# Window attention on one core: row sums and reciprocals behind the value products, row groups innermost

## The reference, cut to what matters

```
x   = x + depthwise3x3(x) + pos_b                      # B, 16, 512, 512
y   = affine1(x) in windows of 8 x 8 pixels            # 16384 windows of 64 tokens, 16 channels
qkv = y @ qkv_w.T + qkv_b ; 2 heads of 8 channels ; q *= 8 ** -0.5
attn = softmax(q @ k.T, axis=-1)                       # 64 x 64 for each window and head
out  = (attn @ v) @ proj_w.T + proj_b
x    = x + out
x    = x + gelu(affine2(x) @ fc1_w.T + fc1_b) @ fc2_w.T + fc2_b    # 64 hidden channels
```

## Time and profile before

| | us |
|---|---|
| median of 3 runs | 33319.02 (33314.83 to 33333.28) |
| the profiled execution's own time | 33304.16 |
| its span, first to last instruction | 33302.7 |
| attention stage, up to its last table load | about 7773 of the span |
| PE, DVE, ACT, POOL busy in the whole span | 30263.7, 27134.7, 24424.2, 11786.8 |

### The profile page before, as it was taken

How to read it: one execution, slowest core, us unless ns; L and a number is a source line. 1 busy time by engine, 2 the same in 40 slices (tenths; PEclk the granted TensorE clock), 3 DMA queues, 4 the chain that set the end, 5 groups by cost and what they waited for, 6 DMA issues and landing times. The chain is left out here.

```text
span 33302.7 us, 708247 instructions
## 1 busy us (share of the span) xinstructions
PE 30263.7 (91%) x264406; PEld 14087.6 (42%) x264406; DVE 27134.7 (81%) x28269; ACT 24424.2 (73%) x25873; POOL 11786.8 (35%) x10892
## 2 busy tenths in 40 slices
PE   7888888889998998999899899899989989989999
PEld 5555555554443343343343333343333434433333
DVE  8888888888997998899799799799889979963102
ACT  5666666667997998899799799799889979951010
POOL 2222222223443443444344344344434434431000
PEclk7777777779999999999999999999999999999999
DMA  1111111116998999999899899899999989999757
GB/s 23 20 20 20 19 20 20 20 20 123 175 175 165 175 175 170 169 175 175 165 175 176 165 175 176 165 175 175 174 166 175 175 165 175 175 241 342 234 183 246
DMA packets 2325306, 4877.21 MB, mean 146 GB/s; under 512 B 632480, under 2 KB 764576, under 8 KB 2322464
## 3 DMA queue, kind: packets, MB, share of 16 engines
q0 software_dynamic: 1224320, 3655.97, 61.4%
q1 hardware_dynamic: 945184, 923.44, 10.2%
q10 hardware_dynamic: 154112, 270.62, 2.2%
HBM read 745.98 MB, written 497.03 MB: 37 GB/s over the span
## 5 line engine op out<-in xcount | busy, mean ns | idle before, releaser
L871 PE MATMUL surf_ps<-surf_u,surf_matf 64*64 64x512 f32 x184960 | 20187.8, 594 | 1619.2 <-ACT surf_Cc L918 555.0
L871 PEld LDWEIGHTS surf_ps<-surf_u,surf_matf 64*64 64x64 f32 x184960 | 8267.0, 134 | 13540.9 <-issue 13534.6
L975 POOL DMA_DIRECT2D surf_u<-surf_ds x4080 | 3452.9, 1154 | 3677.5 <-DVE surf_ds L1038 3295.5
L429 POOL TENSOR_TENSOR att_pr<-att_pr,att_rs 128x1024 f32<-128x1024 f32 x1024 | 2083.9, 2055 | 5660.5 <-DVE att_rs L500 5660.5
L1179 PE MATMUL conv_ps<-conv_rows,conv_w 128*96 128x512 f32 x8256 | 3555.1, 593 | 162.9 <-DVE conv_rows L1200 110.9
L1045 DVE SCALAR_TENSOR_TENSOR surf_rH<-surf_Hc,surf_dt_ab,surf_rH 128x1024 f32<-128x1024 f32 x1360 | 1747.1, 1285 | 1955.8 <-ACT surf_rH L901 1556.5
L953 POOL DMA_DIRECT2D surf_Hc<-surf_m x1360 | 1739.2, 1279 | 3668.8 <-DMA surf_Hc<-surf_Ha 3159.3
L968 POOL DMA_DIRECT2D surf_nK<-surf_B x1360 | 1327.5, 976 | 4088.6 <-ACT surf_B L930 3886.9
L926 ACT ACTIVATE surf_p2q<-surf_pq 128x2048 f32<-128x2048 f32 x1360 | 2591.8, 1906 | 133.0 <-DVE surf_pq L1010 126.8
L471 DVE SCALAR_TENSOR_TENSOR att_acc<-att_xin,att_vec,att_acc 128x512 f32<-128x512 f32 x2048 | 2464.2, 1203 | 45.4
L206 PE MATMUL att_t<-att_ident,att_pr 128*128 128x128 f32 x8192 | 1621.7, 331 | 888.7 <-ACT att_pt L329 886.2
(11 more groups left out here) (88 smaller groups left out, 47547.7 us busy)
## 6 DMA issues: line engine op xcount, KB each, us to landing
surf_p2q<-surf_p2q POOLq DMA_DIRECT2D x1360, 512.0 KB, 10.7
surf_Hc<-surf_Ha POOLq DMA_DIRECT2D x1360, 512.0 KB, 12.3
surf_nK<-surf_B POOLq DMA_DIRECT2D x1360, 512.0 KB, 11.7
surf_Hc<-surf_m POOLq DMA_DIRECT2D x1360, 512.0 KB, 9.0
surf_u<-surf_ds POOLq DMA_DIRECT2D x1360, 256.0 KB, 5.4
surf_u<-surf_ds POOLq DMA_DIRECT2D x2720, 128.0 KB, 7.8
conv_rows<-hidden SPq DMA_DIRECT2D x688, 256.0 KB, 4.0
hidden<-conv_outs ACTq DMA_DIRECT2D x688, 192.0 KB, 4.7
```

Source lines behind the costliest of these rows:

```text
L429: pool.tensor_tensor(pr[:, rg], pr[:, rg], rs[:, rg, :].unsqueeze(2).to_broadcast([P, WC * HEADS, N]), ALU.mult).then_inc(norm_done[rg], 1)
L871: mm = pe.matmul(ps[out, t, :], matf[rows, mat, :], u[rows, k, t, off + 2:off + 2 + W], start=(i == 0), stop=(i == len(taps) - 1))
L975: pool.dma_start(u[rows, k, t, 2:W + 2].rearrange("p a w -> p (a w)"), ds[found, t, :], accum_op=ALU.add).then_inc(u_added, 16)
```

## The change

It takes the normalisation of the attention out of the way of the transposes. The transposed `pt` now holds exp without the division; PE forms the row sums from `pt` by products with a constant 0/1 matrix `pick`, ACT forms 1/sum as exp(-ln(sum)), and DVE multiplies the value products by it. DVE's `total` and all of GpSimd's work are gone, the value products stand in one run with the row group innermost, `pt` has room for two whole chunks, `out_rows` for two stores, the loop body holds four slots, and the order of the steps on PE, ACT and DVE is a new one. The bias of the values goes through the projection once, ahead of the loop (`b_out`).

```diff
-        mx, sm, rs = sb("mx", [P, RG, WC * HEADS]), sb("sm", ...), sb("rs", ...)
-        pt = sb("pt", [P, 2, WC, P])
+        mx = sb("mx", [P, RG, WC * HEADS])
+        pt = sb("pt", [P, 2, RG, WC, P])
+        pick = sb("pick", [P, 2, P // RG])
+        rec = sb("rec", [P, T])
-        out_rows = sb("out_rows", [P, WS, 2 * CW])
+        out_rows = sb("out_rows", [P, 2, WS, 2 * CW])
-        TURNS = [(1, 0), (0, 0), (0, 1), (1, 1), (3, 0), (2, 1), (2, 0), (3, 1)]
+        TURNS = [(1, 0), (0, 0), (0, 1), (1, 1), (3, 1), (2, 1), (3, 0), (2, 0)]
# every_slot
-            for i in range(-2, 5):
-            with eng.Fori(5, CHUNKS - 3, 2) as i:
+            for i in range(-2, 9):
+            with eng.Fori(9, CHUNKS - 3, 4) as i:
+                for k in range(4):
+                    slot(i + k, (1 + k) % 4)
# PE
             def turn(i, rg, half):
-                pe.wait_ge(norm_done[rg], i + 1)
+                pe.wait_ge(exp_done[rg], i + 1)
-            def values(i, par, p):
-                pe.wait_ge(t_copied, i * 8 + (p * 4 + 4))
+            def values(i, par):
+                pe.wait_ge(t_copied, i * 8 + 8)
+                pe.wait_ge(v_split, i + 1)
+                wait(pe, o_done, i)
                 for w in range(WC):
                     for r in range(2):
-                        for rg in (2 * p, 2 * p + 1):
+                        for rg in range(RG):
                             mm = pe.matmul(ps_o[32 * rg:32 * rg + 32, w * N:(w + 1) * N],
                                            vx[:, par, r, w, rg].rearrange("p a h d -> p (a h d)"),
-                                           pt[:, rg % 2, w, r * N:(r + 1) * N], start=(r == 0), stop=(r == 1))
+                                           pt[:, par, rg, w, r * N:(r + 1) * N], start=(r == 0), stop=(r == 1))
+            def sums(i, par):
+                pe.wait_ge(t_copied, i * 8 + 8)
+                after(pe, (gelu_done[1], i - 1), (k_split, i + 1))
+                for r in range(2):
+                    for rg in range(RG):
+                        mm = pe.matmul(ps_mm[32 * rg:32 * rg + 32, 0, :], pick[:, r, :],
+                                       pt[:, par, rg, :, r * N:(r + 1) * N], start=(r == 0), stop=(r == 1))
+                mm.then_inc(den_made, 1)
+            def slot(i, turn4):          # PE, the new order
+                value(i - 1, o); turn(i - 1, 2, 1); scores(i, par, 0); fc1(i - 2, par, 0)
+                turn(i - 1, 3, 0); fc1(i - 2, par, 1); turn(i - 1, 2, 0); scores(i, par, 1)
+                sums(i - 1, o); turn(i, 1, 0); values(i - 1, o); turn(i, 0, 0)
+                project(i - 1); turn(i, 0, 1); fc2(i - 2, par); turn(i, 1, 1)
+                query(i + 1, o); turn(i, 3, 1); key(i + 1, o)
# ACT
-            def move_o(i):               # o_sb = ps_o + bias
+            def reciprocals(i):
+                act.wait_ge(den_made, i + 1)
+                wait(act, o_done, i)
+                act.activation(rec[:, :], ps_m[0], ACT.Ln).then_inc(ln_done, 1)
+                act.wait_ge(ln_done, i + 1)
+                act.activation(rec[:, :], rec[:, :], ACT.Exp, scale=-1.0).then_inc(rec_made, 1)
+            def slot(i, turn4):          # ACT, the new order; the table is now that of ln and exp
+                exps(i - 1, 2); move_t(i - 1, o, 0, 1); move_t(i - 1, o, 1, 1); split_q(i, par)
+                move_t(i - 1, o, 3, 1); split_k(i, par); move_t(i - 1, o, 2, 1); split_v(i - 1, o)
+                gelu(i - 2, par, 0); to_rows(i - 3, (turn4 - 3) % 4); move_t(i - 1, o, 3, 0)
+                gelu(i - 2, par, 1); act.preload_act_table_set("natural_log_exp_and_others")
+                move_t(i - 1, o, 2, 0); exps(i, 1); exps(i, 0); move_t(i, par, 1, 0)
+                reciprocals(i - 1); exps(i, 3); move_t(i, par, 0, 0)
# GpSimd: the whole block with norm() is gone
# DVE
-            def total(i, p):             # sums and reciprocals of two row groups
+            def divide(i):
+                dve.wait_ge(rec_made, i + 1)
+                dve.wait_ge(pv_made, i + 1)
+                wait(dve, proj_made, i)
+                dve.tensor_tensor(o_sb[:, :], ps_o[:, :], rec[:, :], ALU.mult).then_inc(o_done, 1)
+            def slot(i, turn4):          # DVE, the new order
+                conv(i + 1, o, range(5, 7)); top(i, 1); top(i, 0); top(i, 3); top(i, 2)
+                divide(i - 1); conv(i + 1, o, range(7, 8)); residual(i - 1, o)
+                conv(i + 1, o, range(8, 10)); finish(i - 2, par); conv(i + 2, par, range(0, 5))
```

More of the change, by code:

```diff
@@ L229, in fc1 @@
                     pe.wait_ge(x2_done, i + 1)
[L230 to L235, removed]
+                    after(pe, (k_split, i + 2), (y_done, i - 1))
+                    after(pe, (v_split, i + 1))
                 else:
@@ L245, in query @@
                 pe.wait_ge(conv_step, (i + 1) * STEPS_OF_CONV)
-                wait(pe, q_split, i)
-                if there(i - 2):
-                    pe.wait_ge(x2_done, i - 1)
+                after(pe, (x2_done, i - 2), (q_split, i - 1))
                 pe.matmul(ps_m[1], w_qkv[:, 0, :], xs[:, par, :], start=True, stop=True).then_inc(q_made, 1)
@@ L253, in key @@
                     return
-                wait(pe, k_split, i)
-                if there(i - 3):
-                    pe.wait_ge(y_done, i - 2)
+                after(pe, (y_done, i - 3), (rec_made, i - 2), (k_split, i - 1))
                 pe.matmul(ps_m[0], w_qkv[:, 1, :], xs[:, par, :], start=True, stop=True).then_inc(k_made, 1)
@@ L262, in value @@
                     return
[L263 to L266, removed]
+                after(pe, (q_split, i + 1), (x2_done, i - 1))
                 for w in range(WC):
@@ L287, in project @@
                     return
-                pe.wait_ge(o_copied, i + 1)
-                wait(pe, gelu_done[1], i)
+                pe.wait_ge(o_done, i + 1)
+                after(pe, (gelu_done[1], i - 1), (v_split, i))
                 pe.matmul(ps_m[1], w_proj[:, :], o_sb[:, :], start=True, stop=True).then_inc(proj_made, 1)
-            def slot(i, par):
+            def slot(i, turn4):
+                par = turn4 % 2
                 o = 1 - par
+                value(i - 1, o)
+                turn(i - 1, 2, 1)
+                scores(i, par, 0)
+                fc1(i - 2, par, 0)
+                turn(i - 1, 3, 0)
+                fc1(i - 2, par, 1)
+                turn(i - 1, 2, 0)
+                scores(i, par, 1)
+                sums(i - 1, o)
                 turn(i, 1, 0)
+                values(i - 1, o)
+                turn(i, 0, 0)
                 project(i - 1)
+                turn(i, 0, 1)
                 fc2(i - 2, par)
-                turn(i, 0, 0)
+                turn(i, 1, 1)
                 query(i + 1, o)
-                turn(i, 0, 1)
+                turn(i, 3, 1)
                 key(i + 1, o)
[L301 to L312, removed]
             every_slot(pe, slot)
@@ L421, in _ @@
[L421 to L438 removed]
+                exps(i - 1, 2)
@@ new lines, in slot @@
+                move_t(i - 1, o, 0, 1)
+                move_t(i - 1, o, 1, 1)
+                split_q(i, par)
+                move_t(i - 1, o, 3, 1)
+                split_k(i, par)
+                move_t(i - 1, o, 2, 1)
+                split_v(i - 1, o)
+                gelu(i - 2, par, 0)
+                to_rows(i - 3, (turn4 - 3) % 4)
+                move_t(i - 1, o, 3, 0)
+                gelu(i - 2, par, 1)
+                act.preload_act_table_set("natural_log_exp_and_others")
+                move_t(i - 1, o, 2, 0)
@@ L518, in finish @@
                                          op0=ALU.add, op1=ALU.add).then_inc(y_done, 1)
-            def slot(i, par):
+            def slot(i, turn4):
+                par = turn4 % 2
                 o = 1 - par
+                conv(i + 1, o, range(5, 7))
+                top(i, 1)
+                top(i, 0)
+                top(i, 3)
+                top(i, 2)
+                divide(i - 1)
                 conv(i + 1, o, range(7, 8))
-                top(i, 2)
                 residual(i - 1, o)
@@ L573, in attention_weights @@
         ident=np.eye(128, dtype=f),
+        pick=np.stack([(((p[:, None] // 64) == (np.arange(32) // 8) % 2) & (np.arange(32) // 16 == r)).astype(f)
+                       for r in range(2)], axis=1),
         vec=vec)
```

146 lines of the change are left out of this document (57 added, 89 removed).

## The result

| | us |
|---|---|
| before, median of 4 runs beside it | 33316.93 |
| after, median of 4 runs | 32525.28 (32504.89 to 32535.9) |
| ratio | 0.9761, 95% interval 0.9744 to 0.9778 |
| forecast and range | 32,180; 31,600 to 32,950 |

The kernel is 792 us faster, where 1134 were forecast. All of it is in attention: from the first residual step to the last there are 255 slots, which take 26.99 us each instead of 30.09 (start to start of the residual). That is 789 us less. What follows behind the last residual takes 25,545 us after and 25,544 before.

The account below looks back on a forecast made before the run. DVE was taken to bound the 30.08 us slot; after the change, a chain of 23.55 us plus 1.8 (clock) and 0.3 (loop) gives 25.65, saving 1134 us over 256 slots: 32,180 us, range 31,600 to 32,950.

Parts of the forecast that it names:

- The likeliest case: Attention: PE's clock falls in some slots, taken as one in three; 31,850 to 32,550 us, chance 0.42.
- the rival that gave 32,990: Attention: PE's clock falls in every slot, slot 28.8 us, 330 us saved; 32,550 to 33,200, chance 0.22.
- DVE's work: Attention, per slot: falls from 26.4 to 18.2 us, so DVE is no longer the bound.
- The taps: DVE's convolution taps: 0.74 us each instead of 1.207 once GpSimd's operations go, 3.7 us a slot less.
- Value products: PE: 128 instructions with four column groups taking turns take 3.0 us, between 1.9 and 3.8.
- Sums: PE's new row sums: 16 instructions take 1.9 us at full clock and about 3.7 at half.
- The chain: Attention: dependent steps from one chunk's first scores to the next's give the slot, 23.55 us, between 23.1 and 24.3.
- DVE's branch: Chain, after the second scores: DVE's tops 3 and 2 end at 14.35 us, PE's sums and values 0.35 later.
- the walk: Step-by-step count of the chain at full clock, with 0.05 to 0.1 us per signal; 23.55 us a slot.
- The table load: ACT: a load takes 1.28 us, no draining counted, and does not wait for the product behind which its gelu stands.
- The clock: PE's gaps of 0.75 and 1.2 us drop the clock in one slot of three, costing 5.2 us: +1.8 a slot.
- The loop: PE's loop of four slots may wait for instructions: 0 to 0.7 us a slot, 0.3 taken.

Follow-up runs that it names:

- e6: e5 with two products that nobody reads added on PE, ahead of the second fc1 pass and the second scores; 31456 us, 22.84 us a slot.
- e5: e1 with the gelu table asked for explicitly ahead of the first gelu's waits in every slot of ACT; 32073 us, 24.51 us a slot.
- e1: The changed kernel with PE's loop body holding two slots instead of four; 32107 us, 24.71 us a slot.
- e3: e1 with pt laid out so that the 512 moving columns of each row-sum product are contiguous; 32121 us, 24.71 us a slot.
- e8: The kernel before without row sums, reciprocals and GpSimd's normalisation, order of steps unchanged; 32587 us, 27.26 us a slot.

## Why the prediction was right, and where it was off

The sign and the range held; the forecast was 345 us too optimistic. The likeliest case (clock down in some slots, up to 32,550) held by 25 us only, and by luck: it assumed a clock that falls in one slot of three, and the clock fell in nearly every slot, as in the rival that gave 32,990, but for a much shorter time. By the prediction's own steps:

- *DVE's work*: 18.2 us forecast, 2721/147 = 18.5 measured. The taps at 0.74: 0.75. Right. ACT 19.0: 18.6.
- *Value products*: 3.0 us taken, 1.99 measured, at my lower bound. Four column groups do run side by side. The Trainium skill's floor of about 25 ns from start to start ("TensorE: Matmul & The Clock Gate", "Wait — 56ns, not 53.3ns?") does not hold here: 128 instructions in 1.99 us are 15.5 ns apart.
- *Sums*: 1.9 us at full clock and 3.7 at half were both right (1.92 in e6, 3.59 after); I had them at full clock in two slots of three.
- *The chain*: 23.1 us with DVE's branch binding, 22.8 measured in e6, where the clock is full and PE's branch short. DVE waits for nothing at the divide there, as the walk says for that bound. (The walk's own numbers give 23.2: 23.55 less the 0.35 by which PE's branch is later.)
- *The table load*: no draining showed. In e6 a load starts at 5007.86, takes 1.28, and the copy behind it starts at 5009.16. That a load does not wait for the product ahead of its gelu was true of the row that I read, and not of one slot in ACT's loop of four (e5).
- *The clock*: +1.8 us a slot forecast, as one slot in three with a long low stretch. Measured, e5 against e6: 1.67. That the sizes agree is luck, since the form was wrong: with the gaps of 0.62 and 1.27 us the clock falls in nearly every slot, often only for as long as the sums last, and not in one slot of three for 5.2 us. (5.2/3 is 1.7, not 1.8, and the low end of the cost, 1.75 + 1.8 + 0.5, is 4.05, not 4.3.)
- *The loop*: this is the term that was mis-sized. 0.3 us a slot was forecast, with 0.7 as the bound; it was 2.28 (after against e1). I took the surface stage's one idle time of 2.8 us. Here two came, of 2.25 and 2.62 us in the slot shown, 1.22 us a slot in place of 0.7. And I counted no clock behind them, although I had written that PE's idle times bring it down; that is the other 1.06 us. Without the loop term the slot is 24.71 against 25.35 forecast.

22.84 (e6) + 1.67 for the clock behind the gaps + 0.20 for gelu's table + 2.28 for the loop = 26.99. Against the forecast's 25.65 the loop is 1.98 us too low and the chain 0.71 too high, which hid about a third of the miss. The values' overcharge of 1.0 us accounts for only 0.35 to 0.45 of the 0.71, since by the walk DVE's branch binds once the values are short.

With the loop, the table and the gaps mended, the changed kernel takes 31,456 us: 1852 less than the kernel before beside it, more than twice what the change gave as it stood.

## What to carry to other kernels

When a loop on PE is unrolled, look at its return afterwards. Instruction packets in steady state and waits for "issue" behind the return were here the sign that the body had become too long, and the price was the idle time and nearly as much again in clock. Read the durations of one group beside the granted clock of the same stretch before you explain them by layout; e3 was spent on that. Where PE has short gaps in a chain of its own, products that nobody reads can keep the clock: here they gave 1.67 us of 24.51 a slot. And look for the wait that stands in the slow slots only: in e8 it was a store.

## What the runs showed of the hardware that I had not expected

- A loop body of two slots on PE shows no instruction packet in steady state, one of four slots 275 in 2500 us; two idle times, of 2.25 and 2.62 us in the slot shown, stand at its return.
- With gaps of 0.62 and 1.27 us on PE the granted clock fell to 1.2 GHz in every slot of e5; with 0.26 and 0.34 us left of them (e6) it was 1.00 from 500 to 5900 us.
- The same surface stage took 21,959 us in e5 and 21,789 in e6, which differ only in PE instructions that stand ahead of it. Why is open.
- A convolution tap on DVE took 748 ns alone and 2271 ns with GpSimd's normalisation beside it throughout.
- 16 products with 32 columns of weights and 512 moving ones take 1.92 us, and 128 with 64 moving ones 1.99, in four column groups; in two, 3.58.
